# Cross-attention and a mixture of experts on one core: the first scores between the halves of the Q projection, and projections spread over three query blocks

## The reference

```python
x = x + xattn(layernorm(x), ctx, Wq, Wkv, Wout)     # 16 heads of 32
x = x + moe(layernorm(x), ...)                      # 8 experts, top 2, width 352, and a shared one of width 704

# xattn
qp = q @ Wq.T;  k, v = split(ctx @ Wkv.T)
scores = where(causal, q_h @ k_h.T / sqrt(32), min)
out = (softmax(scores) @ v_h) -> heads side by side -> @ Wout.T
# moe
combine = top2(softmax(x @ gate.T))
y = sum_e combine_e * (silu(x @ G_e) * (x @ U_e)) @ D_e + shared expert
```

## Time and profile before

| | us |
|---|---|
| median of 3 runs | 338.91 (337.8 to 339.03) |
| the profiled execution | 337.44 |
| its span, first to last instruction | 335.5 |
| PE busy | 322.2 (96%) |
| DVE busy | 269.9 (80%) |
| ACT busy | 231.2 (69%) |
| POOL busy | 145.6 (43%) |
| mean granted clock of TensorE | 0.995 |

### The profile page before, as it was taken

How to read it: one execution, slowest core, us unless ns; L and a number is a source line. 1 busy time by engine, 2 the same in 40 slices (tenths; PEclk the granted TensorE clock), 3 DMA queues, 4 the chain that set the end, 5 groups by cost and what they waited for, 6 DMA issues and landing times.

```text
span 335.5 us, 7041 instructions
## 1 busy us (share of the span) xinstructions
PE 322.2 (96%) x2285; PEld 278.7 (83%) x2285; DVE 269.9 (80%) x681; ACT 231.2 (69%) x578; POOL 145.6 (43%) x151
## 2 busy tenths in 40 slices
PE   7999998999999999999999999999999999999990
PEld 6898887777786798989888988899889999999980
DVE  4879999999756278857657998999999999999940
ACT  4666999999845135131235788888899899989830
POOL 3335485887843000343400005678863522432463
PEclk9999999999999999999999999999999999999998
DMA  7999400000004799798699674554645455445244
GB/s 231 381 337 380 151 3 3 3 3 0 3 2 185 266 341 371 295 301 282 225 307 263 186 263 93 124 123 86 116 90 133 87 100 128 111 92 110 53 49 47
DMA packets 32226, 53.03 MB, mean 158 GB/s; under 512 B 7488, under 2 KB 15808, under 8 KB 31168
## 3 DMA queue, kind: packets, MB, share of 16 engines
q1 hardware_dynamic: 24912, 43.31, 38.9%
q0 software_dynamic: 4576, 9.23, 15.6%
q10 hardware_dynamic: 2704, 0.04, 0.6%
HBM read 32.24 MB, written 16.92 MB: 147 GB/s over the span
## 4 chain that ended last, share of the span: by engine, by line
PE 78%; DVE 6%; ACT 6%; DMA 3%; POOL 3%; issue 3%; POOLq 1%; DVEq 0%; ACTq 0%; SPq 0%
PE bank L590 31%; PE bank L916 23%; PE bank L943 5%; PE bank L646 3%; ACT prob L1079 3%; PE bank L947 3%; PE bank L810 2%; PE bank L957 2%; PE bank L953 2%; PE bank L796 2%; PE bank L657 2%; PE bank L582 1%; DVE bn L1320 1%; POOL rstd L460 1%; DMA act_w<-act_e 1%
## 5 line engine op out<-in xcount | busy, mean ns | idle before, releaser
L569 POOL DMA_INDIRECT out<-y_sb,dest x18 | 41.5, 2305 | 89.7 <-ACT y_sb L1256 47.2
L1333 DVE TENSOR_TENSOR gu_parts<-w_gu,gu_parts 128x704 fp32r<-128x704 f32 x84 | 76.1, 941 | 0.6 <-ACT gu_parts L1034 0.6
L1034 ACT ACTIVATE gu_parts<-w_gu 128x704 fp32r x84 | 66.2, 793 | 11.2 <-PE bank L916 10.4
L916 PE MATMUL bank<-gu_parts,xsT_hi 128*128 128x352 f32 x328 | 71.0, 338 | 0.0
L916 PEld LDWEIGHTS bank<-gu_parts,xsT_hi 128*128 128x128 f32 x328 | 54.3, 188 | 5.4 <-issue 4.1
L916 PE MATMUL bank<-gu_parts,xsT_lo 128*128 128x352 f32 x164 | 39.6, 323 | 0.0
L590 PE MATMUL bank<-x2T_hi,w_sg_lo 128*128 128x512 f32 (+1 forms) x88 | 32.6, 371 | 0.1
L590 PE MATMUL bank<-x2T_hi,w_sg_hi 128*128 128x512 f32 (+1 forms) x88 | 32.0, 363 | 0.0
L590 PE MATMUL bank<-x2T_lo,w_sg_hi 128*128 128x512 f32 (+1 forms) x88 | 31.9, 363 | 0.0
L452 POOL TENSOR_TENSOR prob<-prob,rrow 112x448 f32<-112x448 f32 x30 | 27.5, 933 | 8.9 <-DVE rrow L1383 8.9
L530 POOL DMA_INDIRECT xs_dram<-x2n,slot_i x14 | 14.2, 1017 | 36.2 <-DVE eid L1637 32.2
(11 more groups left out here) (219 smaller groups left out, 827.2 us busy)
## 6 DMA issues: line engine op xcount, KB each, us to landing
w_gu<-guT SPq DMA_DIRECT2D x8, 1408.0 KB, 9.5
xs_dram<-no_row SPq DMA_DIRECT2D x1, 5460.0 KB, 19.9
xs_in<-xs_dram SPq DMA_DIRECT2D x21, 256.0 KB, 2.9
w_dn<-dnT SPq DMA_DIRECT2D x8, 512.0 KB, 6.7
act_w<-act_e SPq DMA_DIRECT2D x19, 176.0 KB, 2.1
w_sg<-sguT SPq DMA_DIRECT2D x10, 256.0 KB, 5.4
w_dn<-dnT SPq DMA_DIRECT2D x8, 192.0 KB, 7.5
w_sd<-sdnT SPq DMA_DIRECT2D x5, 256.0 KB, 4.9
```

What stands on the lines that cost most here:

```text
L569: pool.indirect_dma_start(out=out[:, :], out_offset=bass.IndirectOffsetOnAxis(ap=dest[:, i, 0:1], axis=0), in_=y_sb[i % 2][:, :], in_offse ...
L916: ins = pe.matmul(dst[:, 0:F], xsT[x_][:, c, :], gu2[w_][:, c, f0:f0 + F], start=c == 0 and n == 0, stop=c == C - 1 and n == 2)
L1034: act.activation(dst, src, ACT.Copy).then_inc(s[sem], 1)
L1333: dve.tensor_tensor(lo_, src, hi_.bitcast(F32), ALU.subtract).then_inc(s[sem], 1)
```

## The change

- **Q's first half is copied out early.** ACT copies columns `first` of each chunk as soon as they are there (`put_qT_part`, new semaphores `Qf` and `QTf`), and later columns `second`. scores(0) and scores(1), whose columns are in the first half, wait for `QTf` alone, and scores(0) are put between chunks 0 and 1 of the second half. ACT's and DVE's work on block 0 (exps, masked) is put between the copies and splits of tiles 4 to 6. t1(4), t1(5), t1(6) go to banks A, B and D instead of S[0] to S[2].
- **apply1 of tiles 5 and 6** goes from DVE to POOL (`xn_p`).
- **All normalisations of block 0 are on POOL**, and DVE's own `normalised` is gone; the copy of (0, 3) goes from DVE to ACT.
- **Projections for k = 1 are spread over three blocks**: q_proj(1, 0), k_proj(1, 1) and q_proj(1, 1) between transposed(0, 1) and (0, 2); q_proj(1, 2) behind scores(2) and ahead of transposed(1, 0); k_proj(1, 2) behind transposed(1, 1), k_proj(1, 3) behind transposed(1, 3); q_proj(1, 3) behind scores(3), ahead of transposed(2, 0). Their copies move on ACT and DVE.
- **The output weights' splits** on POOL: no wait for the down weights, wo_hi in pairs between the normalisations of block 0, wo_lo one at a time in blocks 0 and 1.
- **To the end of the attention on DVE**: the split of the first down weights (`sd_lo(0)`) and the cast of the identity.
- **The tail**: aT_lo(19) ahead of gu_lo(e_next, 20, 3).

```diff
@@ POOL
-            pool.wait_ge(s["wsd_lo"], 1)
-            pool.wait_ge(s["wo"], 16)
-            for c in range(C):
+            def apply1(n):
+                pool.wait_ge(s["T1"], n - 1)
+                pool.wait_ge(s["rs1b"], n + 1)
+                pool.tensor_scalar(xn[n % 2][:, :], xres[:, n, :], mv1[:, n, 0:1], rstd1[:, n, :],
+                                   ALU.subtract, ALU.mult).then_inc(s["xn_p"], 1)
+
+            for n in range(BLK + 1, NX):
+                apply1(n)
...
+            normalised(0, 0)
+            normalised(0, 1)
+            wo_hi(0)
+            wo_hi(1)
+            normalised(0, 2)
+            wo_hi(2)
+            wo_hi(3)
+            normalised(0, 3)
...
-            for c in range(C // 2):
-                wo_lo(c)
-            normalised(0, 2)
             for b in range(NB):
-                normalised(b, 3)
-                if b == 1:
-                    for c in range(C // 2, C):
-                        wo_lo(c)
+                if b >= 1:
+                    normalised(b, 3)
+                if b < 2:
+                    wo_lo(2 * b)
                 if b + 1 < NB:
                     normalised(b + 1, 0)
+                if b < 2:
+                    wo_lo(2 * b + 1)
+                if b + 1 < NB:
                     normalised(b + 1, 1)
@@ PE
             for j in range(C):
+                pe.wait_ge(s["QTf"], j + 1)
                 for c in range(C):
                     ins = q_part(c, j, second, bank[4 + j])
                 ins.then_inc(s["Q"], 1)
+                if j == 0:
+                    scores(0)
                 if j == 1:
-                    t1(4, S[0])
+                    pe.wait_ge(s["QT"], 1)
+                    t1(4, A)
                 if j == 2:
-                    t1(5, S[1])
-                    t1(6, S[2])
+                    pe.wait_ge(s["QT"], 2)
+                    t1(5, B)
...
             k_proj(1, 0, CC)
-            pe.wait_ge(s["xnT_hi"], NX)
-            pe.wait_ge(s["xnT_lo"], NX)
-            scores(0)
-            q_proj(1, 0, D)
-            q_proj(1, 1, B)
+            pe.wait_ge(s["QT"], C)
+            t1(6, D)
@@ PE, in block b, behind the scores
+                if b in (1, 2):
+                    pe.wait_ge(s["QT"], C + b + 1)
+                    q_proj(1, b + 1, D)
+
+                transposed(b, 0)
+                transposed(b, 1)
                 if b == 0:
+                    pe.wait_ge(s["xnT_hi"], NX)
+                    pe.wait_ge(s["xnT_lo"], NX)
+                    q_proj(1, 0, D)
                     pe.wait_ge(s["KT"], C + 1)
                     k_proj(1, 1, CC)
-
-                transposed(b, 0)
-                if b == 0:
-                    pe.wait_ge(s["QT"], C + 2)
-                transposed(b, 1)
-                if b == 0:
-                    q_proj(1, 2, D)
+                    pe.wait_ge(s["QT"], C + 1)
+                    q_proj(1, 1, D)
                 if b == 1:
-                    pe.wait_ge(s["QT"], C + 3)
-                    q_proj(1, 3, D)
-                    pe.wait_ge(s["KT"], C + 3)
+                    pe.wait_ge(s["KT"], C + 2)
                     pe.wait_ge(s["oT_hi"], 1)
                     pe.wait_ge(s["oT_lo"], 1)
-                    k_proj(1, 3, CC)
+                    k_proj(1, 2, CC)
                 if b >= 2:
                     pe.wait_ge(s["QT"], C * NBLK)
...
                 transposed(b, 3)
-                if b == 0:
-                    pe.wait_ge(s["KT"], C + 2)
-                    k_proj(1, 2, CC)
+                if b == 1:
+                    pe.wait_ge(s["KT"], C + 3)
+                    k_proj(1, 3, CC)
@@ ACT
+            for j in range(C):
+                put_qT_part(j, first, "Qf", "QTf")
             ctx_hi(1)
-            for j in range(C):
-                put_qT(0, j, bank[4 + j])
...
+            put_qT_part(0, second, "Q", "QT")
+            sg_hi(0)
+            sd_hi(0)
+            exps(0, 0)
+            put_qT_part(1, second, "Q", "QT")
+            put_xnT(4, A)
+            exps(0, 1)
+            put_qT_part(2, second, "Q", "QT")
+            put_xnT(5, B)
+            put_qT_part(3, second, "Q", "QT")
+            put_xnT(6, D)
+            exps(0, 2)
+            put_kT(1, 0, CC)
+            put_pT(0, 0)
+            put_pT(0, 1)
+            exps(0, 3)
             for b in range(NB):
-                put_pT(b, 0)
-                if b == 0:
-                    put_pT(b, 1)
+                if b == 1:
+                    put_qT(1, 2, D)
+                if b >= 1:
+                    put_pT(b, 0)
@@ DVE
+            stats1(6)
+            dve.wait_ge(s["const"], 3)
             apply1(4)
-            stats1(6)
-            apply1(5)
+            masked(0, 0)
+            masked(0, 1)
             ctx_lo(1)
-            apply1(6)
...
+            masked(0, 2)
+            xnT_lo(4, A)
+            inverse(0, 0)
+            masked(0, 3)
+            xnT_lo(5, B)
+            inverse(0, 1)
+            xnT_lo(6, D)
+            masked(1, 0)
+            inverse(0, 2)
+            masked(1, 1)
             sg_lo(0)
...
+            put_qT(0, D)
             inverse(0, 3)
-            masked(1, 1)
             masked(1, 2)
             for b in range(NB):
-                if b == 0:
-                    put_qT(2, D)
+                if b < 2:
+                    put_kT(b + 1)
                 if b == 1:
-                    put_kT(3)
                     put_pT(1, 3)
                 if b + 1 < NB:
                     inverse(b + 1, 0)
-                if b == 0:
-                    put_pT(0, 3)
-                    put_kT(2)
+                if b == 2:
+                    put_qT(3, D)
                 if b >= 2:
                     put_pT(b, 1)
                 if b + 1 < NB:
                     masked(b + 1, 3)
                 if b == 1:
-                    put_qT(3, D)
+                    put_kT(3)
                 if b + 1 < NB:
                     inverse(b + 1, 1)
+                if b == 0:
+                    put_qT(1, D)
...
+            sd_lo(0)
             sg_lo(1)
             sd_lo(1)
+            dve.tensor_copy(ident_f[:, :], ident[:, :]).then_inc(s["idf"], 1)
@@ DVE, experts' loop
                     if i == NT - 2:
                         dn_lo_part(e, i, 0)
                         dn_lo_part(e, i, 1)
+                        aT_lo(i)
                     gu_lo(e_next, i + 1, 3)
```

74 lines of the change are left out of this document (28 added, 46 removed).

## The result

The changed kernel is slower, and by more than was forecast. Its median is 343.48 us (341.91 to 346.24, four runs) beside 338.55 us (337.8 to 339.03) for the kernel before on the same chip: ratio 1.0155, 95% interval 1.012 to 1.0191. The forecast was 341.8 us, +2.9 on its own base; +4.9 was measured, and the ratio that 341.8 stands for, 1.0085, lies outside the interval. The profiled execution is the slowest of the four: 346.24 us, span 344.1, mean granted clock 0.988, where that of before had 0.995. In this profile the lines are called: L607 (projections; L590 before), L665 (transposes; L646), L679 (scores; L657), L823 (PV; L796), L943 (gate/up; L916), L970 and L974 (down; L943 and L947), L1061 (ACT's copies; L1034), L1110 (exponentials; L1079), L1370 (DVE's splits; L1333), L1431 and L1435 (copies of Q and K; L1402 and L1405).

What follows compares the result with a forecast made beforehand. ACT was taken to bound the attention's query blocks, its lag on entering block 3 carried onward. Terms -0.4 (tail) and +3.3 (ACT late) gave +2.9 us: 338.91 + 2.9 = 341.8 us; 8-in-10 range 337.5 to 343.6.

Steps and rivals of the forecast that it cites:

- the term of 3.3: Entry to block 3: ACT late by 3.3 us, exps(3,2) starting at 58.36 against 55.03.
- the lock between the engines: DVE and POOL slowing each other, as w_sg split against w_o casts: counted as nothing; full-lock rival +1.3 us, 343.1, chance 0.1.
- What bounds it, and that the lag is carried: Attention's query blocks: ACT sets the period; its lead or lag entering block 3 carries through the rest of the kernel.
- The head: Up to block 1: early scores fill ACT's hole, PE nearly full; exps(1,1) at 37.0 against 38.70, lead 1.7 us.
- The K copies: Block 1: PE idles about 1.9 and 0.6 us behind DVE's K copies; PV(1) at 47.55, PE's lead gone.
- The Q copy behind an exponential: Block 2: out_proj(0) waits for DVE's Q copy behind inverse(3,0); PE stands about 2.6 us, ACT waits 2.3.
- The rival by which only block 2's chain costs: Head without unforced idle, transposed(2,0) at about 49, exps(3,2) 0.8 us late: 339.3 us, no change; chance 0.2.
- The other meeting that the prediction named: Head: DVE's ctx_lo(1) against apply1 on POOL (2.08 us), landing in slack of 0.2 us.
- The tail: Last but one tile's down projection: aT_lo(19) ahead of the last gate/up split gains 0.4 us, at worst 0.
- ACT keeps its lead: Rival for blocks 1 and 2: short waits, ACT stays bound and carries its 1.7 us gain: 336.8 us; chance 0.17.
- The upper end: Top of the 8-in-10 range for the whole kernel, 343.6 us, with 1.3 us kept for the lock.

Runs made afterwards that it cites:

- q_copy_early: Changed kernel with DVE's copy of Q's chunk (1,3) between masked(3,1) and masked(3,2) instead of behind inverse(3,0): 340.02 us, ratio 1.0049.
- q3_in_block2_only: Kernel before with only q_proj(1,3) moved to block 2 behind scores(3), its DVE copy behind inverse(3,0): 341.02 us, ratio 1.011.
- kq_and_sg_later: Changed kernel with DVE's copies of K and of Q's chunk (1,3) earlier, and its w_sg split behind masked(1,3): 338.2 us, ratio 1.0004.
- best: As kq_and_sg_later, with TensorE's transposed(0,2) also moved ahead of q_proj(1,1): 337.56 us, ratio 0.9984.

## Why the prediction was right or wrong

The forecast was +2.9. At full clock +3.7 was measured, and the rows add up to it: 3.8 late at exps(3,2), less 0.4 in the tail, and 0.25 outside the span. Two steps failed: the term of 3.3 was 0.5 too small, with the lock between the engines taken at nothing in it, and the clock had no term at all.

**What bounds it, and that the lag is carried: right.** 5.37 us late at exps(3,2), 5.47 at gate_up(0); at full clock 3.96 and 4.02. No idle time was found between that takes any of it back.

**The head: right in kind, 0.4 short.** Scores(0) at 20.60 (forecast 20.6), exps(0,0) at 22.82 (23), exps(1,1) at 37.34 (37.0); from the common point the lead there is 1.3 and not 1.7. The sum by which transposed(1,1) ends at 42.4 took the same matmuls to cost the same in another order, but for 1.7 us of idle time in the old one and 2.1 in the new one. In the trace the idle times are 0.54 (PE busy 22.85 of the 23.39 us from 19.21 to 42.60) and 1.16 (22.64 of 23.80, from 19.05 to 42.85): 0.6 more and not 0.4. And the matmuls, one K projection fewer, took 22.64 where 22.85 - 0.62 = 22.23 was due: 0.4 more, and why stays open.

**The K copies: right in kind, 0.6 too large.** 1.53 + 0.34 of idle time against 1.9 + 0.6; PV(1) at 47.90 against 47.55, since transposed(1,1) ended later than 42.4, at 42.85.

**The Q copy behind an exponential: right, and the largest term.** Idle 2.25 against 2.6, ACT's wait 2.12 against 2.3 at full clock. q_copy_early took the copy out of this cycle and got 3.5 us back; q3_in_block2_only put it alone into the old kernel and lost 2.9 at exps(3,2) from the common point. The rival by which only block 2's chain costs, 339.3, fell: the head leaves PE its idle time too (transposed(2,0) came at 52.00 and not at 49), and the chain alone costs not 0.8 but those 2.9.

**The lock, taken at nothing: a step that failed.** It was 0.64 (1.86 against 1.22), and it lay on the path: masked(1,1), the split and the Q copy for which PE waited 0.88 follow one another on DVE without a gap. With the split as short as before, q_proj(1,1) would have started 0.64 earlier and its wait would have been about 0.24, an estimate from these rows. The forecast had 0.8 for that wait without any lock, so its agreement with 0.88 is luck, two errors that cancel. The landmarks behind it are late against the forecast by about the lock's size at full clock: first w_o matmul 55.37 against 54.85, exps(3,2) 58.99 against 58.36, or 0.4 and 0.5 counted from the common point. No run takes the lock alone out. kq_and_sg_later moves the whole split away and gets 0.8 back. The other meeting that the prediction named did not happen: ctx_lo took 0.62, the same as in the kernel before, though POOL was all the while in its two passes (4.17 together). The Trainium skill, "SBUF — State Buffer", section "Who interferes with whom", lets only one of VectorE and GpSimd hold the port pair that they share, and for a whole instruction. The split beside the casts agrees with it (1.86, near 1.22 and one cast of 0.59, and POOL's two casts 2.17 where the pair before them took 1.17), and so does the split in kq_and_sg_later (2.14, near 1.22 + 0.94); ctx_lo beside the tensor_scalar doesn't, by its 0.62. A range of 3.1 to 4.2 by that rule holds the 3.6 at which gate_up(0) and the tail stand at full clock (4.02 - 0.42), and the sum without it doesn't; but as the 0.8 shows, that is partly luck.

**The clock: a term that was missing, the other step that failed.** The sum was made at full clock, and said in so many words that PE would stand for 2.6 us, but not what the clock does then. In 7 of 16 executions the mean clock has a fall, seen behind that wait in both that were profiled, at 1.6 to 1.7 us each; of the result's four executions two have it, and their median lies between the two kinds. At full clock the changed kernel has 341.96, 3.7 above the kernel before's 338.28. That this is within 0.2 of the forecast's 341.8 is luck: the forecast stood on 338.91, the median of three executions, 0.6 above that of the 74; over all executions its three comparisons have it 4.9, 4.0 and 5.6 above the kernel before on the same chip.

**The tail: right.** 0.42 against 0.4, the same in two kernels.

**ACT keeps its lead: no.** By its own point (PE's idle under 1.5 us from 19.2 on) it was lost at the K copies; with the waits taken out one by one, best has a lead of 0.8 at block 3, not 1.7.

**Chances.** Slower by over 0.5%, given 0.61, came. 343.48 lies inside the range of 337.5 to 343.6 by 0.1, but only because the kernel before was measured 0.4 faster this time: as a change, the upper end is 343.6 - 338.91 = 4.7, a ratio of 1.0138, and 4.9, a ratio of 1.0155, lies above it. The upper end was made for the lock alone (1.3) and had nothing for the clock.
